# An expert kernel whose row transfers on GpSimd are written out with constant tile numbers

## The reference, cut to what matters

```
x = x + ffn(cond(x, cond_128))         # x: 64 x 32 x 512, so 2048 tokens of 512 numbers
cond: per batch row a 32 x 32 mixing matrix from a small network on cond_128, applied to x
ffn, on the 2048 mixed tokens xt:
    scores = softmax(xt @ router_w + router_b) + router_bias      # 16 experts, in 4 groups
    of the 2 groups with the highest score, the 2 experts with the highest score per token
    y = sum over a token's 2 experts of score * ((silu(xt@w1+b1) * (xt@w2+b2)) @ w3 + b3)
    z = (silu(xt@sw1+sb1) * (xt@sw2+sb2)) @ sw3 + sb3             # shared, all tokens
```

## Time and profile before

| what | us |
|---|---|
| three runs | 282.87, 289.75, 286.74 |
| their median | 286.74 |
| span of the profiled execution (first to last instruction) | 282.6 |
| the run nearest to that span | 282.87 |
| share of the span: PE, DVE, POOL, ACT | 90%, 53%, 45%, 28% |

### The profile page before, as it was taken

How to read it: one execution, slowest core, us unless ns; L and a number is a source line. 1 busy time by engine, 2 the same in 40 slices (tenths; PEclk the granted TensorE clock), 3 DMA queues, 4 the chain that set the end, 5 groups by cost and what they waited for, 6 DMA issues and landing times.

```text
span 282.6 us, 4281 instructions
## 1 busy us (share of the span) xinstructions
PE 253.3 (90%) x1092; PEld 163.0 (58%) x1093; DVE 150.1 (53%) x314; ACT 78.6 (28%) x169; POOL 126.0 (45%) x204
## 2 busy tenths in 40 slices
PE   7959889899999859999999889889988979999975
PEld 6826667688864436677775455545555544444421
DVE  0497988569799763344333322332233130179894
ACT  2213455303164002333433232223322221000400
POOL 7673445310111456565656556565656565000160
PEclk9977999999999999999999999999999999999999
DMA  7996876882639359533443343434344433799963
GB/s 224 328 402 217 296 249 205 319 328 121 223 113 420 137 157 369 178 116 119 141 133 121 117 112 107 124 103 148 111 119 140 139 124 118 241 390 388 395 255 148
DMA packets 20699, 57.91 MB, mean 205 GB/s; under 512 B 2533, under 2 KB 2533, under 8 KB 20428
## 3 DMA queue, kind: packets, MB, share of 16 engines
q1 hardware_dynamic: 15084, 39.89, 39.2%
q0 software_dynamic: 5600, 17.83, 19.7%
HBM read 40.94 MB, written 17.30 MB: 206 GB/s over the span
## 4 chain that ended last, share of the span: by engine, by line
PE 38%; issue 26%; POOL 18%; DVE 12%; POOLq 3%; DMA 2%; ACT 0%
PE psum L560 36%; POOL late_region L486 12%; DVE r L959 3%; POOL from_slot L483 3%; DVE xT L1189 2%; POOL to_slot L493 2%; DVE xT L954 2%; DVE xT L928 2%; PE psum L603 2%; DVE xT L969 1%; POOL expert_rows L497 1%; DMA late_region<-xt_rows,from_slot 1%; DMA xT<-cond_pack 1%; DVE mix_bias L956 1%; POOLq L480 1%
## 5 line engine op out<-in xcount | busy, mean ns | idle before, releaser
L560 PE MATMUL psum<-wexp,r 128*128 x272 | 70.2, 387 | 2.1 <-issue 1.2
L560 PEld LDWEIGHTS psum<-wexp,r 128*128 128x128 f32 x272 | 47.1, 190 | 28.9 <-issue 22.8
L928 DVE TENSOR_TENSOR r<-psum,ebias 128x256 f32<-128x256 f32 x34 | 14.4, 425 | 82.5 <-PE psum L560 82.5
L486 POOL DMA_INDIRECT late_region<-xt_rows,from_slot x36 | 36.7, 1019 | 28.5 <-POOL from_slot L483 25.3
L497 POOL DMA_INDIRECT expert_rows<-late_region,to_slot x34 | 34.0, 1001 | 30.1 <-POOL to_slot L493 28.3
L560 PE MATMUL psum<-wexp,xt_sb 128*128 x68 | 36.7, 621 | 7.9 <-issue 7.9
L560 PE MATMUL psum<-xT,shared_sb 128*128 128x512 f32 x64 | 28.0, 593 | 0.8 <-issue 0.8
L871 ACT ACTIVATE late_region<-psum 128x512 f32<-128x512 f32 x34 | 20.3, 597 | 29.5 <-PE psum L560 29.5
L865 ACT ACTIVATE r<-r 128x128 f32<-128x128 f32 x34 | 10.5, 309 | 60.2 <-DVE r L928 60.2
L706 PE MATMUL psum<-ident,late_region 128*128 128x128 f32 x144 | 22.3, 277 | 3.6 <-DMA late_region<-xt_rows,from_slot 3.5
L1145 DVE COPY r<-psum 128x512 f32<-128x512 f32 x36 | 24.6, 684 | 1.5 <-PE psum L706 1.3
(11 more groups left out here) (175 smaller groups left out, 327.7 us busy)
## 6 DMA issues: line engine op xcount, KB each, us to landing
wexp<-expert_pack SPq DMA_DIRECT2D x16, 768.0 KB, 5.2
wexp<-expert_rows SPq DMA_DIRECT2D x8, 1024.0 KB, 13.0
xt_rows<-xt_sb SPq DMA_DIRECT2D x16, 256.0 KB, 2.5
x_early<-x SPq DMA_DIRECT2D x2, 1024.0 KB, 9.0
late_region<-x SPq DMA_DIRECT2D x2, 1024.0 KB, 13.7
ebias<-expert_bias SPq DMA_DIRECT2D x1, 2048.0 KB, 7.2
out_dram<-x_early SPq DMA_DIRECT2D x8, 256.0 KB, 9.8
shared_sb<-shared_pack SPq DMA_DIRECT2D x1, 1536.0 KB, 16.7
```

Of the source, the lines that this page charges most:

```text
L486: nc.gpsimd.indirect_dma_start(out=xg[:, slot, :], out_offset=None, in_=xt_dram[:, :], in_offset=bass.IndirectOffsetOnAxis(ap=from_slot[:, ...
L560: return nc.tensor.matmul(dst, lhsT, rhs, start=start, stop=stop)
L928: return nc.vector.tensor_tensor(dst, a, b, op)
```

## The change

The order of gathers and scatters stays. GpSimd's loop over the certain tiles becomes straight-line code with constant tile numbers, and each transfer there takes its column straight from `from_row` or `to_row`. So for the tiles up to number 35 the copies, the waits for them and the separate wait instructions go. Only tiles beyond that, and the last scatter of all (its number is a register), still copy a column. With 34 tiles, one copy remains.

```diff
+    FAR = SURE + 2
...
-        to_slot = sb("to_slot", [P, RING], I32)
+        to_slot = sb("to_slot", [P, RING + 1], I32)
...
+        last_copied = sem("last_copied")
...
-            def gather(i, slot):
+            def gather_by(column, slot):
+                nc.gpsimd.indirect_dma_start(
+                    out=xg[:, slot, :], out_offset=None, in_=xt_dram[:, :],
+                    in_offset=bass.IndirectOffsetOnAxis(ap=column.bitcast(U32), axis=0),
+                ).then_inc(xg_loaded[slot], 16)
+
+            def scatter_by(column, slot):
+                nc.gpsimd.indirect_dma_start(
+                    out=y_dram[:, :],
+                    out_offset=bass.IndirectOffsetOnAxis(ap=column.bitcast(U32), axis=0),
+                    in_=y_sb[:, slot, :], in_offset=None, bounds_check=ASSIGN - 1, oob_is_err=False,
+                ).then_inc(scattered[slot], 16)
+
+            def gather(i):
+                gather_by(from_row[:, i:i + 1], i % RING)
+
+            def scatter(i):
+                pool.wait_ge(y_ready, i + 1)
+                scatter_by(to_row[:, i:i + 1], i % RING)
+
+            def gather_ahead(i):
+                pool.wait_ge(xgT_done, i + 3)
+                gather(i + 6)
+
+            def pool_step(i):
+                gather_ahead(i)
+                scatter(i - 1)
...
-                hold(from_copied, i + 1)
-                nc.gpsimd.indirect_dma_start(
-                    out=xg[:, slot, :], out_offset=None, in_=xt_dram[:, :],
-                    in_offset=bass.IndirectOffsetOnAxis(ap=from_slot[:, slot:slot + 1].bitcast(U32), axis=0),
-                ).then_inc(xg_loaded[slot], 16)
...
-            gather_ahead(-2, -2)
-            gather_ahead(-1, -1)
-            gather_ahead(0, 0)
-            pool_step(1, 1)
-            pool_pair(1, 1)
-            with pool.Fori(1, (SURE - 2) // 2) as j:
-                for q in range(2):
-                    pool_pair(j * 2 + q, q)
+            for i in (-2, -1, 0):
+                gather_ahead(i)
+            for i in range(1, 2 * (SURE - 2)):
+                pool_step(i)
...
-            scatter(tiles - 1, 1)
+            hold(y_ready, tiles)
+            nc.gpsimd.tensor_copy(to_slot[:, RING:RING + 1], to_row[:, bass.ds(tiles - 1, 1)]
+                                  ).then_inc(last_copied, 1)
+            pool.wait_ge(last_copied, 1)
+            scatter_by(to_slot[:, RING:RING + 1], 1)
```

More of the change, by code:

```diff
@@ L480, in hold, with gather_copied, scatter_copied @@
                 pool.sem_inc(pool_held, 1)
-            def gather(i, slot):
+            def gather_by(column, slot):
[20 more added lines that the diff above has]
+                scatter(i - 1)
+            def gather_copied(i, slot):
+                hold(xgT_done, i - 3)
                 nc.gpsimd.tensor_copy(from_slot[:, slot:slot + 1], from_row[:, bass.ds(i, 1)]
                                       ).then_inc(from_copied, 1)
-                hold(from_copied, i + 1)
-                nc.gpsimd.indirect_dma_start(
-                    out=xg[:, slot, :], out_offset=None, in_=xt_dram[:, :],
-                    in_offset=bass.IndirectOffsetOnAxis(ap=from_slot[:, slot:slot + 1].bitcast(U32), axis=0),
-                ).then_inc(xg_loaded[slot], 16)
-            def scatter(i, slot):
+                hold(from_copied, i - (2 * FAR + 5))
+                gather_by(from_slot[:, slot:slot + 1], slot)
+            def scatter_copied(i, slot):
                 hold(y_ready, i + 1)
@@ L494, in scatter @@
                                       ).then_inc(to_copied, 1)
[L495 to L515, removed]
+                hold(to_copied, i - (2 * FAR - 2))
+                scatter_by(to_slot[:, slot:slot + 1], slot)
             for i in range(RING):
-                gather(i, i)
+                gather(i)
             pool.wait_ge(counts_ready, 1)
             pairs, tiles = count_of(pool, N_PAIRS), count_of(pool, N_TILES)
-            gather_ahead(-2, -2)
@@ L522, in _, with closing_pair @@
-            gather_ahead(-1, -1)
-            gather_ahead(0, 0)
-            pool_step(1, 1)
-            pool_pair(1, 1)
-            with pool.Fori(1, (SURE - 2) // 2) as j:
-                for q in range(2):
-                    pool_pair(j * 2 + q, q)
-            def closing_pair(p, q):
+            for i in (-2, -1, 0):
+                gather_ahead(i)
+            for i in range(1, 2 * (SURE - 2)):
+                pool_step(i)
+            def closing_pair(p):
                 with pool.If(pairs > p + 2):
-                    pool_pair(p, q)
+                    for u in range(2):
+                        pool_step(p * 2 + u)
@@ L532, in closing_pair, with closing_pair_copied @@
                 with pool.If(pairs < p + 3):
                     for u in range(2):
-                        scatter(p * 2 + u - 1, (2 * q + u - 1) % RING)
+                        scatter(p * 2 + u - 1)
+            def closing_pair_copied(p, q):
+                with pool.If(pairs > p + 2):
+                    for u in range(2):
+                        gather_copied(p * 2 + u + 6, (2 * q + u + 2) % RING)
+                        scatter_copied(p * 2 + u - 1, (2 * q + u - 1) % RING)
+                with pool.If(pairs < p + 3):
+                    for u in range(2):
+                        scatter_copied(p * 2 + u - 1, (2 * q + u - 1) % RING)
@@ L536, in _ @@
             for q in range(2):
-                closing_pair(SURE - 2 + q, q)
+                closing_pair(SURE - 2 + q)
             for q in range(2):
                 with pool.If(pairs > SURE + q):
-                    closing_pair(SURE + q, q)
-            with pool.If(pairs > SURE + 2):
+                    closing_pair(SURE + q)
+            with pool.If(pairs > FAR):
                 with pool.Fori(1, (PAIRS - SURE) // 2) as j:
@@ L545, in _ @@
                         with pool.If(pairs > p):
-                            closing_pair(p, q)
-            scatter(tiles - 1, 1)
+                            closing_pair_copied(p, q)
+            hold(y_ready, tiles)
[3 more added lines that the diff above has]
+            scatter_by(to_slot[:, RING:RING + 1], 1)
             pool.wait_ge(x_again_loaded, 16 * (NT - EARLY * GT))
```

## The result

The changed kernel takes **258.92 us** (median of 4 runs, 258.04 to 262.3) against 285.28 for the kernel before (4 runs, 282.87 to 289.75). The ratio is **0.9137**, 95% interval 0.909 to 0.9184: 8.6% faster. It is taken over the fast runs alone (without the one of 262.3, for instance), so it is not the quotient of the two medians, 0.9076. The profiled execution has a span of 256.1 us, against 282.6.

The account below looks back on a forecast made before the run. POOL's 4.08 us step was taken to bound the expert loop. Gains of 18.5 (loop) and 0.8 (start) made 19.3 us off, giving 263.6 from the span or 267.4 from the median; the middle, 265.5 us, was forecast, range 260.5 to 275.

Parts of the forecast that it names:

- POOL's pace, and the preparation of a transfer as the greater part of it: Expert loop: POOL's 4.08 us step sets the pace; gaps of 0.79 and 0.89 behind copies outweigh the copies' 0.20 each.
- POOL's floor: Expert loop after the change: POOL's step with preparation covered, forecast at 2.0 to 2.4 us.
- Rival A: Expert loop: preparation is not covered, POOL's step is 3.68 us, gain about 12.8 us, time 270 to 274; chance 10%.
- PE late next, at 3.137 a step: Expert loop after the change: PE becomes the bound for all steps, at 3.137 us each.
- the 18.5 forecast: Expert loop: gain from PE's pace up to tile 35, 18.9 us earlier less 0.4 for a branch.
- The 0.4 taken off for a branch: PE's branch at tile 34, thought hidden behind the wait for the gather: 0.4 us off the loop's gain.
- Transfers hidden: Expert loop: same bytes in less time, DMA share about 0.51, no wait of PE, costed at nothing.
- Rivals B and C: Expert loop: B, slower descriptors from the table column, up to 337 us, 3%; C, transfers become the bound, about 286, 4%.
- The start, 0.8: Start of the expert loop: an earlier first gather without copy and wait was taken to gain 0.8 us.
- 0 to 1.1 us: Start of the expert loop: the range given for what an earlier first tile is worth.
- The end, "all of that moves as a block: 0": Behind the last step: second half of the shared network and the final scatter's wait keep their length, gain 0.
- The time around the span: Whole kernel: profiled span of 282.6 us set against 282.87 us for the nearest run.

Follow-up runs that it names:

- e1: The changed kernel with each column copy and its wait put back just ahead of the transfer: 289.88 us, ratio to before 1.0242.
- e2: The changed kernel with the copies put back, but each made one transfer earlier into a column of its own: 263.63 us.
- e9: The changed kernel with half of each expert's first product left out, so PE's step falls below POOL's: 240.74 us, one run.
- e8: The kernel before with DVE's comparison for the tiles' experts moved ahead of the tables, away from the first gather: 281.67 us, one run.
- e4: The changed kernel with only scatters taking their column from the table, gathers copying it as before: 263.0 us, ratio to before 0.9322.
- e10: The changed kernel run once more, unaltered, on the chip of e7: 259.61 us, ratio to before 0.9129.
- e3: The changed kernel with only gathers taking their column from the table, scatters copying it as before: 260.87 us, ratio to before 0.9236.
- e7: The changed kernel with DVE's comparison for the tiles' experts moved ahead of the tables: 260.48 us, ratio to before 0.9155.

## Why the prediction was right, and where it was not

*POOL's pace, and the preparation of a transfer as the greater part of it:* right. e1 has the whole loss back with constants and straight code in place; e2 loses it again with all copies kept. The overlap that the prediction read from one place, a number load that ran beside a transfer, is the 0.30 between two transfers. POOL's floor was mis-sized, 2.60 where it said 2.0 to 2.4; it did no harm, as both lie under 3.137. Rival A (3.68 a step) is excluded by the rows: a gap of 0.30, and waits for ACT.

*PE late next, at 3.137 a step:* right, to the third digit, and e9 shows it from the other side. The loop gave 19.0 for the 18.5 forecast. The 0.4 taken off for a branch was most of the difference: from tile 6 to tile 35 there are 29 steps of 3.137 and no surplus. The other 0.1 lies ahead of tile 6.

*Transfers hidden:* right. From 148 to 210 us PE was idle for 0.03 of 62.00 us, at a DMA share of 0.45 (forecast 0.51). Rivals B and C did not come: the transfers take 0.97 to 1.01 us as before, and PE never waits for them in the stretch.

*The start, 0.8:* mis-sized, it gave 2.3. The pieces are in the rows. The gather begins 0.30 instead of 1.19 us behind the tables, 0.89. It takes 1.19 instead of 1.94, 0.75. PE's transposes of the first tile thereby come 1.69 earlier, and the product does not wait 0.84 but 0.26 behind them, 0.58 more. The step that failed is "0 to 1.1 us": it bounded the gain by the start of the gather alone and left the duration out of the sum, although it had named the comparison beside it. Its reason for the bound held: DVE copied tile 0 no earlier, 6.35 us behind the tables where it was 6.38. But this copy was not what PE's product waited for before. The Trainium skill (SBUF — State Buffer, Who interferes with whom) has DVE instructions with two SBUF inputs contend with a GpSimd instruction that reads SBUF; e8 agrees, with 0.74 of the 0.96 us that the prediction named.

*The end, "all of that moves as a block: 0":* wrong, by 2.7 us. Behind tile 35, PE before and then PE after:

```profile
230.97 1.12 PE L560 MATMUL psum<-wexp,xt_sb 128*128 x2 [0.49 <-issue]
232.90 1.95 PE L560 MATMUL psum<-xT,shared_sb 128*128 128x512 f32 x4 [0.81 <-issue]
```

```profile
206.43 1.02 PE L580 MATMUL psum<-wexp,xt_sb 128*128 x2
207.49 1.96 PE L580 MATMUL psum<-xT,shared_sb 128*128 128x512 f32 x4
```

From tile 35 to the shared product it was 3.08 us before and is 1.49 now. 1.30 of these 1.59 are the two waits on "issue", time in which PE waited for nothing that the profile shows, just behind a gather that PE had waited for. They go with POOL's pace: e1 and e8, in which PE still waits for gathers at the end of the loop, have 0.87 and 0.89 us ahead of the shared product, while the kernel after, e2, e4 and e10, in which it doesn't, have none. That PE's sequencer is what was late there is my reading; no run shows it apart. The prediction saw PE busy from 235 us on the earlier trace rows and took the 5 us ahead of that for part of the block. The remaining 1.1 us are nearly all in one place of the last stage: DVE's eight sums of 128x512 from 263.00 us on, beside a product of GpSimd, take 7.56 us before and 6.53 in the kernel after. Runs with the same code there have either value (6.52 in e4 and e10, 7.59 in e3, 7.53 in e7), so I don't give them to the change.

*The time around the span.* The prediction took 0.27 us, from a span and a run that do not belong together; the runs that came with the result show 1.9 (258.04 us for a span of 256.1). With the span of 282.6 this makes the profiled execution some 284.5, not 282.87, and the same sum 265.2: the middle that the prediction chose between its two readings was right by this. In the profiled pair that is 265.2 against 258.04, and the miss of 7.2 us is start, end and loop (1.5 + 2.7 + 0.5) and the earlier tables (2.5). The unexplained spread of 6.9 us between the runs of the kernel before goes at least in part with the clock: of its later runs on one chip one took 281.94 us at a mean granted clock of 1.00 and one 289.8 at 0.964. In the profiled executions the clock from 14 to 30 us came at 0.69 to 1.00; the four at 1.00 had their tables at 92.5 to 93.2 us, the eight below it at 93.7 to 98.5. Not all of that is the clock, as the first piece above shows.

## What to carry to other kernels

Set the step of the engine that issues the transfers, with its gaps, beside PE's step, stretch by stretch: a busy share of 45% can be a bound, since a sequencer's preparation does not count as busy. If an instruction must be fed a column or a number, make it at least one instruction earlier, or read it where it lies; a cheap copy right ahead of its reader costs more in lost overlap than in its own time. When a late engine is made early, look for what else stood behind the lateness (here waits of PE for nothing that the profile shows, and a collision with DVE): these small terms all had the same sign.

## What the hardware showed that I had not expected

- Two indirect transfers on GpSimd follow each other after 0.30 us; behind a copy of their column it is 0.79 (gather) and 0.89 (scatter).
- In the rows below (kernel after) ACT's result is there at 113.05 + 0.60, and the scatter that waits for it begins 0.80 us behind. The gather of 115.90 waits for PE's transposes of tile 6, which end at 115.03 + 0.60, and begins 0.27 behind. So it looks as if a gather's preparation lies ahead of its wait and a scatter's does not; the ends of PE's instructions are modelled in the profile, so the 0.27 is rough. The scatter has a bounds check, which the gather has not; whether that is the cause wasn't tried.

```profile
113.05 0.60 ACT L891 ACTIVATE late_region<-psum 128x512 f32<-128x512 f32 x1 [0.41 <-PE psum L580]
...
114.45 1.01 POOL L491 DMA_INDIRECT expert_rows<-late_region,to_row  x1 [0.84 <-ACT late_region L891]
...
115.90 0.97 POOL L485 DMA_INDIRECT late_region<-xt_rows,from_row  x1 [0.44 <-PE psum L726]
```

- DVE's comparison of 128x768 with two inputs lengthened the first gather from 1.20 us (e8) to 1.94 when both began within 0.1 us of each other, and not when the gather was 0.8 us ahead (1.19). The same comparison took 1.75 instead of 0.95 beside GpSimd's product.
